# The normalised tiles of an attention and expert kernel brought to the matmul layout by transposing DMAs

## The reference, cut to what matters

```python
def xattn(h, adj_raw, Wq, Wk, gamma_raw):          # h = ctx (4,512,128), adj_raw = layernorm(x)
    sim = einsum('bhnd,bhmd->bnm', Q, K) / (sqrt(d) * H)
    threshold = top_k(sim, int(n * 0.3))[0][:, :, -1:]
    A = sigmoid(sim) * (sim >= threshold)
    A = (A + swapaxes(A, -1, -2)) * 0.5
    return (1 - sigmoid(gamma_raw)) * adj_raw + sigmoid(gamma_raw) * A
x = x + xattn(ctx_512, layernorm(x), ...)          # x (4,512,512)
xn = layernorm(x)
# router: softmax(xn @ router_w.T), the best 2 of 8 experts, weights normalised
# experts: silu(xn @ gate) * (xn @ up) @ down, width 352
# shared:  silu(xn @ s_gate + b) * (xn @ s_up + b) @ s_down + b, width 704
x = x + experts + shared
```

## Time and profile before

| | us |
|---|---|
| median of 3 runs | 588.96 (588.16 to 589.74) |
| the profiled execution | 589.12 |
| its span, first to last instruction | 587.3 |

### The profile page before, as it was taken

One profiled execution on the slowest core, in us unless ns is written; L12 is line 12 of the kernel. 1 busy time (PEld: TensorE's weight loads), 2 busy tenths in 40 slices (PEclk: granted clock), 3 DMA queues, 4 the chain that ended last, 5 costly groups with the idle time before them and its releaser, 6 DMA issues.

```text
span 587.3 us, 9556 instructions
## 1 busy us (share of the span) xinstructions
PE 478.6 (81%) x2914; PEld 269.9 (46%) x2915; DVE 341.8 (58%) x890; ACT 236.0 (40%) x417; POOL 196.2 (33%) x247
## 2 busy tenths in 40 slices
PE   5220539979799869976898989999999999999970
PEld 2000324434343434433445546666666666666640
DVE  1699787688677976785299365545545533223210
ACT  3552265443654374443443244444444432222220
POOL 0012245004300070004219433544454454544531
PEclk9765769999699988998699799999999999999985
DMA  5701240004700162005333295677688745454451
GB/s 139 247 18 36 90 144 19 1 0 128 179 1 1 71 133 83 1 1 145 73 99 104 86 266 174 158 208 188 163 199 181 171 74 94 83 89 90 75 91 18
DMA packets 36926, 60.51 MB, mean 103 GB/s; under 512 B 6153, under 2 KB 16649, under 8 KB 36882
## 3 DMA queue, kind: packets, MB, share of 16 engines
q0 software_dynamic: 10384, 23.34, 21.9%
q1 hardware_dynamic: 26498, 36.60, 19.6%
HBM read 37.64 MB, written 22.28 MB: 102 GB/s over the span
## 4 chain that ended last, share of the span: by engine, by line
PE 61%; DVE 20%; ACT 6%; issue 6%; DMA 3%; POOL 3%; DVEq 0%; SPq 0%; ACTq 0%; POOLq 0%
PE bank L925 5%; PE bank L926 5%; PE bank L927 5%; PE bank L1068 4%; PE bank L1070 4%; PE bank L1069 4%; PE bank L1044 4%; PE bank L1048 3%; PE bank L1046 3%; PE bank L1047 3%; PE bank L1049 3%; PE bank L1045 3%; PE bank L1030 3%; PE bank L871 2%; PE bank L1057 2%
## 5 line engine op out<-in xcount | busy, mean ns | idle before, releaser
L925 PE MATMUL bank<-xT,W 128*128 128x512 f16 x176 | 69.8, 397 | 0.0
L926 PE MATMUL bank<-xT,W 128*128 128x512 f16 x176 | 69.8, 396 | 0.0
L927 PE MATMUL bank<-xT,W 128*128 128x512 f16 x176 | 69.5, 395 | 0.0
L562 POOL DMA_INDIRECT out_dram<-xb,sidx x35 | 56.8, 1624 | 29.7 <-POOL sidx L561 28.6
L1438 DVE TENSOR_TENSOR hS<-bank,hS 128x384 f16<-128x384 f32 x35 | 19.5, 558 | 73.4 <-ACT hS L804 67.3
L798 ACT ACTIVATE sgt<-bank 128x352 f32<-128x352 f32 x35 | 16.2, 463 | 86.2 <-PE bank L1049 86.2
L1433 DVE SCALAR_TENSOR_TENSOR xb<-bank,sgt 128x352 f32<-128x352 f32 x35 | 18.4, 525 | 54.7 <-ACT sgt L798 54.7
L492 POOL TENSOR_TENSOR rstd<-pw 128x4 f32<-128x4 f32 x12 | 12.5, 1042 | 107.4 <-DVE pw L1149 107.1
L812 ACT ACTIVATE xb<-bank,wcol 128x512 f32<-128x512 f32 x35 | 24.1, 688 | 56.8 <-PE bank L1070 55.3
L937 PE MATMUL bank<-W,hS 128*128 128x512 f16 x96 | 37.1, 387 | 10.8 <-DVE hS L1303 9.4
L1044 PE MATMUL bank<-W,xT 128*128 x140 | 43.8, 313 | 0.2 <-issue 0.2
(11 more groups left out here) (230 smaller groups left out, 1082.5 us busy)
## 6 DMA issues: line engine op xcount, KB each, us to landing
xn_dram<-xn SPq DMA_DIRECT2D x17, 256.0 KB, 2.0
xb<-x_in SPq DMA_DIRECT2D x4, 1024.0 KB, 6.4
out_dram<-xb SPq DMA_DIRECT2D x16, 256.0 KB, 2.6
out_dram<-ysh POOLq DMA_DIRECT2D x12, 256.0 KB, 4.1
stage<-L_ffn_down_w_in SPq DMA_DIRECT2D x12, 256.0 KB
sim<-L_ffn_down_w_in SPq DMA_DIRECT2D x12, 256.0 KB
stage<-L_ffn_gate_w_in SPq DMA_DIRECT2D x16, 176.0 KB
stage<-L_ffn_up_w_in SPq DMA_DIRECT2D x16, 176.0 KB
```

The lines of the kernel that those rows point to most:

```text
L925: pe.matmul(o, wh, xT[:, 0, c, :], start=(c == 0), stop=False)
L926: pe.matmul(o, wh, xT[:, 1, c, :], start=False, stop=False)
L927: last = pe.matmul(o, wl, xT[:, 0, c, :], start=False, stop=(c == KD - 1))
```

## The change

`xn` gets four places, one for each tile of a batch, in the columns of `W` that belong to expert place 1. `transpose_xn` on TensorE and `x_T` on ScalarE go. Instead SP issues one transposing DMA per tile, from `xn` straight to `xT`, as soon as the tile's remainder is there; the first of a batch also waits for shared up of the batch before, as `x_T` did. SP's four writes to `xn_dram` come behind the four transposes. TensorE's `logits` waits for the transposes tile by tile. `xn_hi` no longer waits within a batch; it waits for the write and the transpose of the same place in the batch before. `ylast` becomes a tensor of its own.

```diff
-    xn = sb("xn", [P, 2, 2 * D], F16)
+    ylast = sb("ylast", [P, 2, D])
+    xn = W[:, EW:EW + TB * 2 * D].rearrange("p (t d) -> p t d", t=TB)
@@ block.sync
             for t in range(TB):
                 g = TB * b + t
                 sp.wait_ge(s_nlo, g + 1)
-                sp.dma_start(xn_dram[g * P:(g + 1) * P, :], xn[:, t % 2, :]).then_inc(d_xn[t % 2], 16)
+                if b and t == 0:
+                    sp.wait_ge(s_gu, SC * b)
+                sp.dma_start_transpose(xT[:, :, :, t * P:(t + 1) * P].rearrange("p s c t -> p (s c) t"), xn[:, t, :]).then_inc(d_xT[t], 16)
+            for t in range(TB):
+                g = TB * b + t
+                sp.dma_start(xn_dram[g * P:(g + 1) * P, :], xn[:, t, :]).then_inc(d_xn[t], 16)
             if b + 1 < NB:
                 sp.dma_start(xb[:, :, :], x[b + 1].rearrange("(t p) d -> p t d", p=P)).then_inc(d_x, 16)
@@ block.scalar
         def xn_hi(b, t):
             g = TB * b + t
             act.wait_ge(s_xn, g + 1)
-            if g >= 2:
-                act.wait_ge(d_xn[t % 2], 16 * (g // 2))
-                act.wait_ge(s_xnT, g - 1)
-            else:
-                act.wait_ge(d_zero, 32)
-            act.activation(xn[:, t % 2, 0:D], xb[:, t, :], ACT.Copy).then_inc(s_nhi, 1)
-
-        def x_T(b, t):
-            ...
+            if b:
+                act.wait_ge(d_xn[t], 16 * b)
+                act.wait_ge(d_xT[t], 16 * b)
+            act.activation(xn[:, t, 0:D], xb[:, t, :], ACT.Copy).then_inc(s_nhi, 1)
@@
-            xn_hi(b, 0)
-            xn_hi(b, 1)
+            for t in range(TB):
+                xn_hi(b, t)
             if b:
                 shared_out(b - 1, 2, ysh[:, 0, :])
-            x_T(b, 0)
-            x_T(b, 1)
-            xn_hi(b, 2)
-            xn_hi(b, 3)
             if b + 1 < NB:
                 count(b + 1, 0)
             if b:
                 shared_out(b - 1, 3, ysh[:, 1, :])
-            x_T(b, 2)
-            x_T(b, 3)
@@ block.tensor
-        def transpose_xn(b, t):
-            ...
         def logits(b):
-            pe.wait_ge(s_xT, TB * (b + 1))
             pe.wait_ge(s_simc, min(TB * (b + 2), NT))
             for t in range(TB):
+                pe.wait_ge(d_xT[t], 16 * (b + 1))
...
-            transpose_xn(b, 0)
-            transpose_xn(b, 1)
-            transpose_xn(b, 2)
-            transpose_xn(b, 3)
             logits(b)
```

More of the change, by code:

```diff
@@ L201, in build @@
     xg = [t[:, :].bitcast(F16) for t in (qT, kT)]
-    ylast = xn[:, :, :].bitcast(F32)
+    xn = W[:, EW:EW + TB * 2 * D].rearrange("p (t d) -> p t d", t=TB)
     ylasts = [ylast[:, 0, :], ylast[:, 1, :], xb[:, 0, :], xb[:, 1, :]]
@@ L271, in build @@
     d_zero = sem("d_zero")
-    d_xn = [sem(f"d_xn{i}") for i in range(2)]
+    d_xn = [sem(f"d_xn{i}") for i in range(TB)]
+    d_xT = [sem(f"d_xT{i}") for i in range(TB)]
     d_y = [sem(f"d_y{i}") for i in range(2)]
@@ L300, in build @@
     s_xn = sem("s_xn")
-    s_xnT = sem("s_xnT")
-    s_xT = sem("s_xT")
     s_lg = sem("s_lg")
@@ L413, in _ @@
         sp.wait_ge(s_zero, 1)
-        sp.dma_start(xn_dram[DUMMY:DUMMY + P, :], xn[:, 0, :]).then_inc(d_zero, 16)
+        sp.dma_start(xn_dram[DUMMY:DUMMY + P, :], ylast[:, 0, :].bitcast(F16)).then_inc(d_zero, 16)
         sp.dma_start(out[DUMMY:DUMMY + P, :], ylast[:, 0, :]).then_inc(d_zero, 16)
@@ L437, in _ @@
         sp.wait_ge(d_x1, 16 * NT)
-        for i in range(2):
-            sp.wait_ge(d_xn[i], 16 * NT // 2)
+        for i in range(TB):
+            sp.wait_ge(d_xn[i], 16 * NB)
         sp.wait_ge(d_zero, 32)
@@ L502, in xn_lo @@
             pool.wait_ge(s_nhi, g + 1)
-            pool.tensor_tensor(xn[:, t % 2, D:2 * D], xb[:, t, :], xn[:, t % 2, 0:D], ALU.subtract).then_inc(s_nlo, 1)
+            pool.tensor_tensor(xn[:, t, D:2 * D], xb[:, t, :], xn[:, t, 0:D], ALU.subtract).then_inc(s_nlo, 1)
         for b in range(NB):
@@ L571, in _ @@
         pool.wait_ge(s_route, 1)
-        for i in range(2):
-            pool.wait_ge(d_xn[i], 16 * NT // 2)
+        for i in range(TB):
+            pool.wait_ge(d_xn[i], 16 * NB)
         pool.wait_ge(d_zero, 32)
@@ L786, in _ @@
             split_some(FIRST_AT[q])
-        act.wait_ge(s_xnT, NT)
-        for i in range(2):
-            act.wait_ge(d_xn[i], 16 * NT // 2)
+        for i in range(TB):
+            act.wait_ge(d_xT[i], 16 * NB)
+            act.wait_ge(d_xn[i], 16 * NB)
         for t in range(TB):
@@ L876, in transpose_A @@
                 pe.wait_ge(s_A, TB * (b + 1))
-                if b:
-                    pe.wait_ge(s_xT, TB * b)
-                else:
+                if b == 0:
                     pe.wait_ge(s_rw, 1)
@@ L913, in shared_up @@
                 pe.wait_ge(s_wloD, EARLY)
-            if q == 0:
-                pe.wait_ge(s_xT, TB * (b + 1))
             if q >= 2:
@@ L1110, in link @@
             dve.wait_ge(s_chain, chain[0])
-        dve.memset(xn[:, 0, :], 0.0).then_inc(s_zero, 1)
+        dve.memset(ylast[:, 0, :], 0.0).then_inc(s_zero, 1)
         def weight_lo(n):
```

## The result

The changed kernel took 594.59 us (median, 590.58 to 596.53), the kernel before beside it 589.41 us (587.25 to 592.29). The ratio is 1.0069 with a 95% interval of 1.004 to 1.0098: slower by 0.4 to 1.0%. The prediction was 595.0 us. The number came out, but two of its terms were off in opposite directions, so that the closeness is luck.

The account below looks back on a forecast made before the run. The prediction took TensorE, 81% busy, as the bound, so only its standing time counts. 589.12 us plus 5.1 for the transposes' path and 1.0 for the clock gave 595.2, 595.0 as the median; range 583 to 618.

Parts of the forecast that it names:

- The start of shared up as the hinge: On TensorE, once per batch: a shift of shared up's start goes 1:1 into the end while VectorE follows.
- Remainders 0.36, 0.44 and 1.04 us sooner: On GpSimd, the wait before tile 2 goes: 0.36, 0.44 and 1.04 us in batches 1 to 3, none in batch 0.
- A piece of 256 B at 33 ns, the engines held 2.5 us: On the DMA engines: 1024 pieces per transpose, 33 ns per added piece, so one transpose holds the engines 2.5 us.
- L = 3.85 us: Transposing DMA's time from issue to landing: 2.0 us of a plain write plus 56 more pieces at 0.033 us.
- q = 1.37 us: Tile 3's transpose queued behind tile 2's: 2.5 us of held engines less 1.13 us between the tiles.
- The clock, 1.0 us: On TensorE, up to 0.97 us more solid work per batch at half speed; bounds 0 and 1.9 us, 1.0 taken.
- about 6 us after the logits' start: TensorE's granted clock reaches 1.00 about 6 us after the logits start, and should still do so in the new profile.
- The late load of `x` at zero: On SP, the next `x` load goes behind transposes and writes; VectorE's later waits cover it; uncovered, up to 3 us a batch.
- Four places bring 0.36 to 1.04 us and cost nothing: In `xn_hi`, ScalarE writes tiles 2 and 3 right behind 0 and 1; new waits on old transfers cost nothing.
- Rival 1: A transpose lands like a plain transfer, L = 2.0 us and q = 0: faster, 582.2 us; chance 0.28.
- Rival 3: Finer pieces, 512 per engine, 3.8 us a transpose, make the DMA engines the bound: 617 us; chance 0.17.
- Rival 4: Eight 128x128 blocks land one after another, 15 us a tile: about 50 us later per batch, near 790; chance 0.05.

Follow-up runs that it names:

- e3: The changed kernel without GpSimd's twelve accumulating writes of batches 0 to 2, that part of the output left out: 582.65 us, ratio 0.988 to the kernel before.
- e2: The changed kernel with unread matmuls filling TensorE's waits for each tile's transpose: 588.97 us, ratio 1.001 to the kernel before.
- e5: The kernel before, with unread matmuls filling TensorE's waits ahead of the transposes and the logits: 583.27 us, ratio 0.9878.
- e1: The kernel before with only the four places and the new order of `xn_hi`, TensorE still transposing: 592.66 us, ratio 1.0055.
- e6: The kernel of e1 with ScalarE's count passes of the next batch moved behind the last evictions: 586.43 us, ratio 0.9952 to the kernel before.
- e8: The kernel before without the same accumulating writes as in e3, same output part left out: 587.75 us, ratio 0.998.
- e4: The changed kernel with the load of the next `x` issued ahead of the writes to `xn_dram`: 593.76 us, ratio 1.0074 to the kernel before.
- e7: The changed kernel with each tile transposed twice by DMA, first into columns nobody reads: 615.41 us, ratio 1.044 to the kernel before.
- e10: The kernel of e2 with other counts of unread matmuls, so the clock holds in batch 3 too: 590.43 us, ratio 0.9995 to the kernel before.
- e12: The kernel of e10 with the next `x` load ahead of the `xn_dram` writes, as in e4: 583.04 us, ratio 0.9862 to the kernel before.
- e11: The changed kernel with each tile's transpose issued as eight DMAs of one 128x128 block: 720.36 us, ratio 1.2221 to the kernel before.
- e9: The kernel of e6 with TensorE's waits filled by unread matmuls: 580.22 us, ratio 0.9841 to the kernel before.

## Why the prediction came out, step by step

- **The start of shared up as the hinge.** Right. The shifts of it and the time behind it add up to the difference of the two traces (the sum under the table), and VectorE followed.
- **Remainders 0.36, 0.44 and 1.04 us sooner.** Right: 0.34, 0.43 and 1.03, counted from the first remainder of the batch. In batch 1, `146.66 2.55 POOL L507` now runs both tiles with no wait.
- **A piece of 256 B at 33 ns, the engines held 2.5 us.** Too high. The trace counts 16,896 more packets, the 1024 pieces of a transpose and 32 more each that I had not listed. In 82.50 to 85.00 of after, 1815 packets filled the engines to 94%, 0.94 x 16 x 2.5 / 1815 = 21 ns a piece, 1.3 us a transpose. The 33 ns came from two transfers that stand in different places of the program and go in different directions, not only in different pieces; the tiny packets' 7.5 ns were too low. The window of after:

```profile
82.50:85.00 2.50, 0.25 (x9) 0.26 (x10) 2.10 (x15) 1.97 (x6) 0.09 (x1) 0.50 0.94 183
```

- **L = 3.85 us.** Right in the middle (3.9), for a reason that I did not have. A transpose lands in 3.1 to 3.3 us in batch 0, where GpSimd issues no accumulating write, and in 3.1 to 3.8 in e3. It is up to 6.0 us beside GpSimd's accumulating writes. I had named the writes in a clause, and given them no price.
- **q = 1.37 us.** This is the term that failed. It was built on the 2.5 us. With 1.3 us held and 1.13 us between the tiles 0.2 us are left of it. From the end of the last remainder to the issue of its transpose the chain shows 0.19, 0.44, 0.46 and 0.30 us in the four batches, of which 0.1 belongs to the term ahead of L. Together with L the path came to 4.64 us on average instead of 5.65, four times 1.0 us: 1.1 us of growth measured where 5.1 stood (with the gains that the sum counted on coming in).
- **The clock, 1.0 us.** Too small, and my upper bound of 1.9 with it: 2.3 us. I reckoned only with 1.30 us of logits that stop being solid work. Before, TensorE had the transposes of tiles 2 and 3 in that stretch as well (2.15 us); after, it has four groups of logits and long waits. That what stands in this stretch decides is shown by e2 and e5, which filled it. That it was these transposes is argued, and the other traces fit: the slow time is 14.2 to 15.2 us in the four kernels with TensorE's transposes and unfilled waits (before, e1, e6, e8) and 17.9 to 19.8 in the four with transposing DMAs (after, e3, e4, e7). No run separates the missing transposes from the longer waits. The rule "about 6 us after the logits' start" does not hold either. In batches 0 and 1 the full clock came at the same moment in both traces (90.7, 159.0), though shared up had moved by -1.80 and +0.66. In batches 2 and 3 it came 3.4 us later, though shared up had moved by 0.65 and 2.52. The rows of 288 show the latter, after (0.64 in the earlier trace rows):

```profile
288.00:289.00 1.00, 1.00 (x4) 0.30 (x3) 0.26 (x2) 0.00 (x0) 0.20 (x1) 0.50 1.03 387
```

- **The late load of `x` at zero.** Right for this kernel, and only for it. VectorE's wait grew from 1.7 to 12.2 us over three batches, 3.5 us each where I had said up to 3, and e4 shows that TensorE felt none of it. It is issued at 155.45 (I had said about 153). My sentence on the lost cover (up to 3 us a batch) is what e10 and e12 then showed: 1.3% or, by the ratios, 7.8 us, some 2.6 a batch (in the traces 5.5 us of it are where the load can act).
- **Four places bring 0.36 to 1.04 us and cost nothing.** The gain was right, the cost was missed. VectorE's `dif` grew to 3.15 us beside the unbroken remainders. I followed the queues past which a step moved, and not what else used the gap that it closed. In the changed kernel nothing of the path stands behind it; in e1 the evictions do, and e1 is 0.55% slower than the kernel before.
- **The rivals.** Rival 1 (lands like a plain transfer) is out: nothing landed under 3.1 us, the plain write's 2.0 was not reached. Rival 3 (finer pieces) is out with 21 ns and 1024 pieces. Rival 4 is out for one DMA of eight blocks; e11 made its blocks follow one another by hand (720.36 us, where the rival gave near 790), by SP's issue and not by landings.

So 5.1 + 1.0 was forecast and 1.1 + 2.3 came in the traces, 4.1 by the ratio. The two errors cancelled in part: 4.0 us too much on the path, 1.3 too little on the clock. That the median nevertheless lies 0.4 us from the forecast is luck. The profiled execution, for which the forecast was 595.2, took 591.85, and the other 2.7 us up to the median come from executions of which there is no trace. What stays open is why the changed kernel's executions without a trace are on average longer than the traced one. Landings that vary with the accumulating writes would do it, and e3 against e8 speaks for it, but no trace of a long execution shows it.

## What to carry to other kernels

Here a transposing DMA did not beat TensorE's transposes while GpSimd's accumulating writes ran: it lost 0.7%, and once TensorE's waits were filled and the load of `x` went first it came level with e5 and not clearly behind e9. If it is used, many blocks belong in one DMA (e11), and its input has to be ready at least 3.1 us before its use. Where its landing ends a wait of TensorE, price it with what else is on the DMA engines then, not alone. Ahead of a long stretch of matmuls, look first at TensorE's clock in the windows: filling the waits with unread matmuls gave 1.2% here (e5), more than the whole change moved. But fit their number to the wait: too many delay what they should help (e2, batch 2). A step that is hidden by another engine's waits is hidden only as long as those waits last, so each time a path gets shorter, ask again what it was covering.

## What the hardware showed that I had not expected

- An SP issue of a transposing DMA takes 1.23 us for 32 KB and 1.33 us for 256 KB, against 0.32 us for a plain one. The Trainium skill (VectorE: DVE Perf Modes, The three transpose paths) gives 1309 ns for a 128x128 block. The trace of e11 agrees for a DMA of one block (1232 ns of SP's time, the median of 128), but eight blocks in one DMA took 1.33 us, so it is not a price per block.
- 256 KB in 1.33 us are 197 GB/s; the window from 82.50 to 85.00 of after shows 183 GB/s with the engines filled to 94%. The Trainium skill (Advanced Engine Details and Errata, X-Bar Transpose (TRN2)) expects 350 to 400 GB/s and the speed of regular DMAs; here the landing was 3.2 us against 2.0. The measurement decides.
- Beside GpSimd's accumulating writes a transpose landed in up to 6.0 us, 3.9 in the middle, without them in 3.8 and 3.2 (after against e3), while taking those writes out of the kernel before changed its time by 0.2%, within its interval.
- VectorE's 128x4 operation with two inputs in SBUF took 3.15 us instead of 0.16 while GpSimd ran two remainders back to back, and it ended with the second. The Trainium skill (SBUF — State Buffer, Terms) has the two engines share a port pair that is held for a whole instruction; the traces agree in part. Where the two remainders follow a power with nothing between, `dif` takes 1.10 us (batch 0 of both kernels, and e3), about one remainder (1.13). It takes 3.15 us, until the second ends, only where GpSimd also issues a DMA ahead of them (after and e1, batches 1 and 2). Why is open: by its record `dif` starts at 146.09, during that issue, and the remainders only at 146.66, and GpSimd's records are rough. The rows of after, and batch 0 of the kernel before:

```profile
146.66 2.55 POOL L507 TENSOR_TENSOR W<-xb,W 128x512 f16<-128x512 f32 x2
```

```profile
146.09 3.15 DVE L1127 TENSOR_TENSOR dif<-mv,rstd 128x4 f32<-128x4 f32 x1 [1.16 <-POOL rstd L496]
```

```profile
80.82 1.10 DVE L1157 TENSOR_TENSOR dif<-mv,rstd 128x4 f32<-128x4 f32 x1 [1.13 <-POOL rstd L492]
```
